# A decoder block on one core: the experts' gate and up weights are loaded and split in eight pieces during the last two batches instead of whole in the first

## The reference

```python
x = x + _L0_attn_ref(_layernorm(x), Win, bin_, Bp, Cp, Dp, Wout, bout)      # silu(x @ Win), scan with decay 0.9
x = x + _L0_xattn_ref(_layernorm(x), ctx_1024, ctx_1024, mask, Wq, ..., bo) # softmax attention
x = x + _L0_ffn_ref(_layernorm(x), router_w, ..., wg, wp, wo)
...
scores = (jnp.einsum('btd,ed->bte', x, router_w) + router_b) / temp
gates = _sinkhorn(scores)                        # 3 rounds of log-sum-exp over experts, then tokens
topk_vals, topk_idx = jax.lax.top_k(gates, K)    # K = 2
g = jax.nn.relu(jnp.einsum('btd,edf->btef', x, wg))
p = jnp.einsum('btd,edf->btef', x, wp)
all_out = jnp.einsum('btef,efd->bted', g * p, wo)
```

## Time and profile before

| | us |
|---|---|
| median of 3 runs (lowest, highest) | 435.16 (434.74, 436.1) |
| the profiled execution's own time | 434.68 |
| its span in the trace | 432.9 |
| busy: TensorE, VectorE, ScalarE, GpSimd | 359.2, 242.1, 151.1, 56.6 |
| mean granted TensorE clock | 0.888 |

### The profile page before, as it was taken

How to read it: one execution, slowest core, us unless ns; L and a number is a source line. 1 busy time by engine, 2 the same in 40 slices (tenths; PEclk the granted TensorE clock), 3 DMA queues, 4 the chain that set the end, 5 groups by cost and what they waited for, 6 DMA issues and landing times.

```text
span 432.9 us, 6018 instructions
## 1 busy us (share of the span) xinstructions
PE 359.2 (83%) x2063; PEld 247.6 (57%) x2063; DVE 242.1 (56%) x682; ACT 151.1 (35%) x300; POOL 56.6 (13%) x85
## 2 busy tenths in 40 slices
PE   1455168749987799779997799999989999999996
PEld 0343136433454535464454445988878888788875
DVE  2373568672297833963279541757567645554553
ACT  3504413705734166005541374223233222222221
POOL 7322131642012130001000200010000000000000
PEclk9866687766997999957899599989999999999999
DMA  4201284601005110151000003000000000000000
GB/s 113 59 12 34 58 197 136 145 6 46 0 2 129 26 44 2 37 115 45 2 0 2 5 2 97 2 0 2 1 26 0 0 26 2 0 2 24 0 0 24
DMA packets 17296, 15.38 MB, mean 36 GB/s; under 512 B 4469, under 2 KB 16693, under 8 KB 16981
## 3 DMA queue, kind: packets, MB, share of 16 engines
q1 hardware_dynamic: 16885, 14.84, 13.6%
q10 hardware_dynamic: 384, 0.20, 0.2%
HBM read 11.72 MB, written 3.11 MB: 34 GB/s over the span
## 4 chain that ended last, share of the span: by engine, by line
PE 69%; DVE 14%; ACT 5%; DMA 5%; issue 3%; ACTq 1%; POOL 1%; SPq 0%; DVEq 0%; POOLq 0%
PE pS L1056 14%; DVE nmax_mask L908 5%; PE pS L1205 5%; PE pS L1202 4%; PE pC L1220 4%; PE pS L253 4%; PE pS L255 3%; PE pS L254 3%; PE pC L1217 3%; PE pA L253 3%; PE pA L254 3%; PE pA L255 3%; PE pB L253 3%; PE pB L255 3%; PE pB L254 3%
## 5 line engine op out<-in xcount | busy, mean ns | idle before, releaser
L1056 PEld LDWEIGHTS pS<-prob,sig 128*128 128x128 f32 x512 | 65.4, 192 | 13.7 <-DVE res L720 6.3
L709 DVE TENSOR_TENSOR sig<-xi_f,pS 128x512 f32<-128x512 f32 x64 | 43.9, 685 | 50.9 <-PE pS L255 46.0
L1056 PE MATMUL pS<-prob,sig 128*128 128x128 f32 x512 | 69.6, 280 | 1.2 <-DVE sig L709 1.0
L908 DVE TENSOR_REDUCE nmax_mask<-pS 128x3 f32<-128x462 f32 (+1 forms) x96 | 52.5, 574 | 12.8 <-PE pS L1178 12.1
L636 ACT ACTIVATE prob<-pS 128x512 f32<-128x512 f32 x80 | 43.9, 597 | 31.7 <-PE pS L1205 31.7
L1175 PE MATMUL pS<-k_stack,q_stack 72*128 72x154 bf16 x256 | 36.8, 251 | 13.3 <-DVE nmax_mask L908 10.2
L720 DVE SCALAR_TENSOR_TENSOR res<-pS,w_gate,res 128x128 f32<-128x128 f32 (+1 forms) x128 | 36.0, 344 | 14.3 <-PE pS L1056 13.4
L553 ACT ACTIVATE xi_f<-pA 128x512 f32<-128x512 f32 x32 | 19.1, 598 | 61.4 <-PE pA L255 61.3
L1175 PEld LDWEIGHTS pS<-k_stack,q_stack 72*128 72x128 bf16 x256 | 21.2, 106 | 32.8 <-DVE nmax_mask L908 23.3
L553 ACT ACTIVATE xi_f<-pB 128x512 f32<-128x512 f32 x32 | 19.1, 598 | 52.5 <-PE pB L255 52.4
L1178 PE MATMUL pS<-mbias,ident_bf 128*128 128x462 bf16 (+1 forms) x96 | 36.4, 380 | 0.0
(11 more groups left out here) (275 smaller groups left out, 647.8 us busy)
## 6 DMA issues: line engine op xcount, KB each, us to landing
q_stack<-q_scr SPq DMA_DIRECT2D x12, 384.0 KB
q_scr<-q_parts SPq DMA_DIRECT2D x12, 128.0 KB, 2.3
k_stack<-k_scr SPq DMA_DIRECT2D x36, 40.0 KB
res<-in_x_dram SPq DMA_DIRECT2D x4, 256.0 KB, 6.3
prob<-in_L_ffn_wg_dram SPq DMA_DIRECT2D x1, 1024.0 KB, 5.9
prob<-in_L_ffn_wp_dram SPq DMA_DIRECT2D x1, 1024.0 KB, 9.6
out_dram<-res SPq DMA_DIRECT2D x4, 256.0 KB, 2.2
prob<-in_L_ffn_wo_dram SPq DMA_DIRECT2D x1, 768.0 KB, 5.0
```

Source lines behind the costliest of these rows:

```text
L709: dve.tensor_tensor(hid[:, i % 2, :], relu[:, i % 2, :], pUp[i % 2][:, :], ALU.mult).then_inc(s_hid, 1)
L908: dve.tensor_reduce(nmax[:, qt, hs[0]:hs[-1] + 1], score_bank(b, n)[:, 0:len(hs) * KEYS].rearrange("p (h k) -> p h k", k=KEYS), AX.X, ALU. ...
L1056: last = pe.matmul(pO[:, toks], hid[:, i % 2, toks], wo_sb[:, e, hf, :], start=(hf == 0 and t == 0), stop=(hf == HF - 1), skip_group_check ...
```

## The change

`wgp_raw` becomes a view of `ctx_in`: 4 KB in each partition, two halves of one piece (two experts of `wg` or `wp`, 256 KB) each. Step `load_experts` loads one piece; piece n goes into half n % 2, and from piece 2 on SyncE waits until piece n - 2 has been split by GpSimd. The loads stand in slots 29, 29, 33, 37, 41, 45 of batch 2 and 2, 6 of batch 3; the splits stand in slots 32, 36, 40, 44 of batch 2 and 1, 5, 29, 33 of batch 3. The first loads of x for batches 2 and 3 stay where they were, in a step `load_x`. The first exponentials no longer wait for the splits.

```diff
+        wgp_raw = ctx_in[:, :, :, :].rearrange("p b i d -> p (b i d)").rearrange("p (n e f) -> p n e f", n=2, f=FF)
...
-        wgp_raw = prob[:, 0:2 * E * FF // S, :].rearrange("p u n -> p (u n)").rearrange(
-            "p (w e f) -> p w e f", w=2, e=E)
...
+        s_wgp = [sem("w_gp_in%d" % i) for i in range(2)]
...
-        EXPERTS_AT = [17, 18, 19, 20, 21, 22, 23, 24]
+        LOAD_AT = ([29, 29, 33, 37, 41, 45], [2, 6])
+        EXPERTS_AT = ([32, 36, 40, 44], [1, 5, 29, 33])
...
-            if b == 0:
-                place([("split_experts", 0, n) for n in range(EXPERT_STEPS)], EXPERTS_AT)
+            if b >= NB - 2:
+                n0 = 0 if b == NB - 2 else 6
+                place([("load_experts", 0, n0 + i) for i in range(len(LOAD_AT[b - NB + 2]))], LOAD_AT[b - NB + 2])
+                place([("split_experts", 0, EXPERT_STEPS // 2 * (b - NB + 2) + i) for i in range(EXPERT_STEPS // 2)],
+                      EXPERTS_AT[b - NB + 2])
...
-                if step == "load_experts":
+                if step == "load_x":
 
                     for i in range(2, NB):
                         sp.dma_start(res[:, i, :, :], x[i].rearrange("(t p) d -> p t d", p=P)).then_inc(s_x[i], 16)
-                    sp.wait_ge(s_qst, 16 * PARTS)
-                    sp.dma_start(wgp_raw[:, 0, :, :], wg.rearrange("e d f -> d e f")).then_inc(s_wgp, 16)
-                    sp.dma_start(wgp_raw[:, 1, :, :], wp.rearrange("e d f -> d e f")).then_inc(s_wgp, 16)
+                elif step == "load_experts":
+                    if n == 0:
+                        sp.wait_ge(s_ctxT, NB)
+                    if n >= 2:
+                        sp.wait_ge(s_wsplit, n - 1)
+                    w, e = divmod(n * EXPERT_STEP, E)
+                    sp.dma_start(wgp_raw[:, n % 2, :, :], (wg, wp)[w][e:e + EXPERT_STEP].rearrange("e d f -> d e f")
+                                 ).then_inc(s_wgp[n % 2], 16)
...
-                    pool.tensor_tensor(wgp[1][:, w, es, :], wgp_raw[:, w, es, :], f32(wgp[0][:, w, es, :]),
+                    pool.tensor_tensor(wgp[1][:, w, es, :], wgp_raw[:, n % 2, :, :], f32(wgp[0][:, w, es, :]),
                                        ALU.subtract).then_inc(s_wsplit, 1)
...
-                    act.wait_ge(s_wgp, 32)
+                    act.wait_ge(s_wgp[n % 2], 16 * (n // 2 + 1))
...
-                    act.copy(wgp[0][:, w, es, :], wgp_raw[:, w, es, :]).then_inc(s_xsplit, 1)
+                    act.copy(wgp[0][:, w, es, :], wgp_raw[:, n % 2, :, :]).then_inc(s_xsplit, 1)
...
-                    else:
-                        act.wait_ge(s_wsplit, EXPERT_STEPS)
```

More of the change, by code:

```diff
@@ L199, in build_decoder @@
         s_ones = sem("ones_ready")
-        (s_wwin, s_wmix, s_wsmall, s_wproj, s_wgp, s_wo, s_wo2, s_mask, s_zero, s_ident, s_identb, s_const,
+        (s_wwin, s_wmix, s_wsmall, s_wproj, s_wo, s_wo2, s_mask, s_zero, s_ident, s_identb, s_const,
          s_bc, s_wsplit, s_xsplit, s_maskb, s_maskT, s_maskTc,
          s_nh, s_cpT, s_rwhi, s_projT, s_projhi, s_proj, s_winhi, s_winsplit, s_mixw, s_kones, s_seg) = (sem(n) for n in (
-             "w_win_in", "w_mix_in", "w_small_in", "w_proj_in", "w_gp_in", "w_o_in", "w_o_rest_in", "mask_in", "zeroed", "ident_ready",
+             "w_win_in", "w_mix_in", "w_small_in", "w_proj_in", "w_o_in", "w_o_rest_in", "mask_in", "zeroed", "ident_ready",
              "ident_bf_ready", "const_ready", "bc_step",
@@ L335, in build_decoder @@
                  + mix_out(0)[3:5] + second[2:4] + mix_out(0)[5:] + second[4:WIN1] + queries(0)[:4]
-                 + second[WIN1:WIN1 + 2] + queries(0)[4:] + [("load_experts", 0, 0)] + second[WIN1 + 2:] + mix_out(1))
+                 + second[WIN1:WIN1 + 2] + queries(0)[4:] + [("load_x", 0, 0)] + second[WIN1 + 2:] + mix_out(1))
         for b in range(NB):
```

## The result

The changed kernel takes **438.22 us** (median of nine runs, 436.26 to 442.85) against 435.16 of the kernel before in the same session: ratio **1.0095, 95% interval 1.0053 to 1.0137**. In a second session it was 438.33 against 435.13, ratio 1.0073 (1.0045 to 1.0100). It is slower, by some 3.1 us. The profiled execution took 438.22, its span is 436.5 against 432.9, and the mean granted clock 0.889 against 0.888.

The account below looks back on a forecast made before the run. TensorE, with 69% of the chain of waits, was taken as the bound. Terms -2.6 + 3.9 + 2.0 + 0.4 + 1.0 = +4.7 on 434.68 gave 439.4, plus 0.5 for the median: 439.9 us, 8-in-10 range 435.4 to 443.0.

Parts of the forecast that it names:

- rival 1: Batch 2: the clock holds through TensorE's stop, sum +2.7 us, 437.9; chance 0.15.
- Rival 2: Batch 0: the shorter stop keeps the clock up, a further gain of 1.9 us, 438.0; chance 0.15.
- Batch 0, -2.6: End of batch 0's max stage: three VectorE instructions no longer held by GpSimd's subtractions, 2.6 us gained.
- Rival 4: Batch 0: the three slow VectorE instructions were held by something else and stay slow, 442.5; chance 0.05.
- Piece 0, +3.9: Batch 2: ScalarE's cast waits for the late first load, delaying TensorE's router matmuls by 3.9 us, bounds 3.0 to 6.0.
- The landing: Batch 2: the first load lands 2.7 us after its issue, at 204.6; bounds 2.7 and 4.5.
- The chain behind the landing: Batch 2: cast, exponential 6, `x_hi`, `x_lo` and hand-over before the router matmuls take 2.4 us.
- The clock, +2.0: Behind the stop in batch 2: lower clock, 24 x (0.20 - 0.116), costs 2.0 us; bounds 0 to 4.
- Pieces 1 to 3, 0: Batch 2: the later casts and loads cost nothing; without cover, one would cost up to 0.6 us.
- Batch 3, +0.4 and +1.0: Batch 3: GpSimd holds VectorE, +0.4 us in the max stage (0 to 2.4), +1.0 in the routing chain (0 to 2).

Follow-up runs that it names:

- experiment 5: The changed kernel run again, unedited: 438.33 us against 435.13 for the kernel before, ratio 1.0073.
- experiment 6: The changed kernel with eight two-input GpSimd subtractions put back into slots 17 to 24 of batch 0: 442.23 us, ratio 1.0165 to the kernel before.
- experiment 1: The changed kernel with the first two loads in slot 16 of batch 2 instead of 29: 437.05 us against 435.37 for the kernel before, ratio 1.0006.
- experiment 4: The changed kernel with the first two loads in slot 16 of batch 2 and the last two splits of batch 3 in slots 38 and 43: 436.22 us, ratio 1.0023.

## Why the prediction was right

Right in sign and mechanism: 439.9 was forecast, 438.22 measured, in the range of 435.4 to 443.0. The number alone would fit rivals 1 and 2 better, which stand at 437.9 and 438.0; it is the traces that decide against them. By its own steps:

- *Batch 0, -2.6.* Measured -2.64, and -2.91 in experiment 5. The cause is shown by experiment 6. Rival 4 falls.
- *Piece 0, +3.9.* Measured +4.83, and +3.60 to +4.13 in the three other profiles with the stop. The landing was under-sized: I took 2.7 from the load of `wo`, and behind nine transfers of keys it was 3.8 and, in the others, 3.0 to 3.2, inside the bounds of 2.7 to 4.5. In these the load was issued 6.4 to 6.8 us behind the first scores, not 7.1, which made up for it, so that +3.80 in experiment 5 is so near to +3.9 is in part luck. The chain behind the landing was forecast at 2.4 and is 2.42 and 2.41.
- *The clock, +2.0.* No run shows this term as it was worked out, 24 x (0.20 - 0.116). The two distances can be read from the kernel before, 2.67 us from the first to the last of the 24 router matmuls and 10 other matmuls in 2.00 us at a clock of 0.50; that the clock would fall behind this stop was an estimate of mine from the stop of 4.09 us in batch 0. What the runs showed in its place: +1.54, and +2.49 to +2.96 in the three other profiles with the stop, all inside the bounds of 0 to 4. In experiment 5 the router matmuls ran at the half level (0.50), 0.21 apart, as forecast. In the profile of the result they ran at the full level (1.00 over 204 to 206; rival 1, for 2 us), and the half level (0.50 over 208 to 212) came behind them and lasted some 3 us longer than before, over score units and a group product. So the term was right in size, and its place differs from one execution to the next. It is a small part of the span, 1.54 of 436.5, but half of the 3.1 us that the change costs in all, so the term belongs in a sum of this size.
- *Pieces 1 to 3, 0.* Nothing waits for them: the second cast stands right behind an exponential, 209.83.
- *Batch 3, +0.4 and +1.0.* In the trace +0.17 and +0.70. `route_log` was held, at 1.09, and two more instructions in the chain than before; most of it was covered. Only 0.4 of the 0.70 stands behind the chain; 0.25 lies ahead of it, in the first score units (5.71 us against 5.46), which is the clock. Both terms were too high.
- *Rival 2.* The clock in batch 0 fell as before, 0.61 over 90 to 92. The shorter stop did not keep it.
- *Not forecast:* -1.04 between the first scores of batches 0 and 2, where the change moves nothing. In experiment 5, the same kernel, it is +0.21, so it is no part of the change. The stretch from the scores of batch 0 to the row of batch 1 is 21.2 there where it is 19.3 in the first profile and 19.7 before, so I put this down to where the clock happened to be low. That is argued, not shown.
- *The working.* The bounds of 3.0 and 6.0 for piece 0 don't follow from its landings of 2.7 and 4.5, which give 3.9 and 5.7. All bounds at their ends give 435.6 and 447.0, so the range of 437.0 to 443.0 takes it that they don't fall together. The last reader of `ctx_in` stands in slot 15, fourteen slots ahead of the load and not twelve. None of this moves the forecast.

The forecast lay 1.7 too high: 1.1 are the terms (3.6 in the trace against 4.7), of which the unforeseen 1.04 is nearly all, since the larger wait and the smaller clock and batch 3 terms cancel; 0.5 is that I added the distance of the median from the profiled execution, which this time was nothing. That the number came so near is in part luck: one kernel's profiles differ by 1 us and more in stretches that the change doesn't touch.

## What to carry to other kernels

A load that is moved close to its use is only as early as its place in the queue. Here piece 0 was issued 6.9 us behind the first scores of batch 2, and landed 3.0 to 3.8 us later with nine transfers of keys in front, where it took 2.7 and 2.6 with none. So read the issue time behind everything in front of the load, and add a landing from a row with the same traffic ahead, not from a quiet one. An engine that walks a list in order makes every later step wait for the one whose input is late: the cast of piece 0 waited 4.40 us, and exponential 6 and the router's cast started behind it, at 202.40 and 202.89. So either issue the load further ahead or put the cast behind the urgent one. The second is one list of slots here, the first two slots and one wait of SyncE; each turned a loss of 0.7 to 0.9% into a gain of 0.4 to 0.5%. Do not issue the load a few us ahead of a small transfer that everything waits for, on another queue either: TensorE's wait there was 3.64 and 2.77 us in experiments 1 and 4, against 0.64 to 1.63 in the ten other profiles. And compare two profiles of the same kernel (here -1.04 and +0.21 us in one stretch) before a difference of 1 us between two kernels is given a cause.

## What was not expected

- A stop that was as long as the idle time says would have been 2.74 us. The delay was 4.83, since the half clock in front of the stop (0.50 over 196 to 198) was hidden in it. Where TensorE worked at half clock in front of the stop, the idle row alone undercounts what a late landing costs against a kernel without it. In experiment 5 the clock was high there, 0.91 over 196 to 198, and the idle time of 3.72 is nearly the whole delay of 3.80.
- Two loads of 256 KB, issued 4.7 us ahead of three transfers of 16 KB on another queue, made these land 4.8 to 5.5 us after their issue, and 4.3 to 5.0 in experiment 4. It is 2.4 to 4.5 in the ten other profiles.
- On GpSimd a 128x512 subtraction of a tile from itself took 1.00 us, and of two tiles 1.235.
- The time of one kernel varies by several us, in part with the clock: experiment 1's twelve runs go from 432.9 to 441.0, with mean granted clocks of 0.90 in the fastest and 0.87 in the slowest. Single profiles of this kernel are compared stretch by stretch for that reason.
- The clock behind a stop in the middle of a kernel cost 1.5 to 3.0 us in the four profiles that have it, a third to four fifths of the delay by the stop itself.
